# First tile of attention and FFN: rows two to four normalised on GpSimd, row four's attention products earlier, ScalarE's splits ahead of a test

## The chip, the core and the metric

The kernel runs on one core of one Trainium2 chip. The metric is the device time of one execution in microseconds (us), median over runs. The core has TensorE (matrix products), VectorE, ScalarE and GpSimd (elementwise work) and SyncE, which here only issues DMAs. The engines run their own instruction lists in order and wait for one another on semaphores.

## The reference

One block over x of 8 x 256 tokens x 256 features, float32:

```
q = layernorm(x)                                   # no learned scale
scores = q @ ctx.T / 16, causal, padded keys masked with -inf
x = x + softmax(scores) @ ctx
n = layernorm(x)
h = silu(n @ w1.T * s1) * (n @ w2.T * s2)          # 256 -> 1024, weights -1, 0, 1
h = gelu(h @ h1.T * sh1);  h = gelu(h @ h2.T * sh2)  # 1024 -> 1024, twice
out = x + h @ w3.T * s3                            # 1024 -> 256
```

## The kernel before, in words

The 2048 tokens are four tiles of 512, each of two sequences of 256. A tile has four "rows" of 128 tokens (r = 0 to 3 in the code; "row one" to "row four" in words); rows 0 and 1 are the first sequence. All 22 weight pieces (128 x 1024 each) stay in SBUF. The FFN's activations are split into a high and a low part, and each weight multiplies both in two matmuls, so the hidden layers take most of TensorE.

The four tiles run one after another on TensorE. In tiles 2 to 4 the attention of the next tile is slipped between hidden chunks. The first tile has nothing to be slipped into, so it has a path written out by hand: the functions whose names begin with `first_`, and the order of their calls on each engine. That order is what the change edits.

For one row of the first tile: statistics of x (`first_stats_of`, `first_moments_of`), deviation, transpose, scores, exponentials, transposed probabilities, the product with the context (`first_attend`, TensorE, line 1180), division by the row sum and addition of x (`first_attention`, VectorE, line 779), statistics and moments again (lines 727, 732), the reciprocal root of the variance on GpSimd (`first_attention_rstd`, lines 402 and 403), normalisation (`first_normalise`, VectorE, line 791), transpose (`first_turn_xn`, TensorE, line 1188), the high part on ScalarE and the low part on VectorE (both `first_split`, lines 510 and 798). Then gate and up products start (`gate_and_up`, line 997). In the first tile the first chunks are done for the first sequence alone (batch 0, 256 columns), then for the second (batch 1). The PSUM banks form a ring of six: chunk 3 needs the banks of chunk 0 and so waits until VectorE has multiplied gate and up of chunk 0 (line 819), which waits for ScalarE's silu (line 549).

Beside that, ScalarE tests every weight piece for bits that a shorter format would lose (`test_piece`, line 466). TensorE sums the test results (`sum_flag`, line 1063), VectorE reduces them to a flag (`take_flag`, line 804), and TensorE's queue loads the flag and branches (`segment`) before the products of the segment: GATE_UP_A ahead of the first product, then GATE_UP_B, HID1A, HID1B, HID1C and LAST. The first six pieces arrive in buffers that are free at first (gate, residual, ctx_cols, work, turned, ctx_rows) and GpSimd copies them into the weights' place (`first_weights`, line 436). SyncE issues raw pieces 4 and 5 when row four's attention product is done (`first_attended[3]`), the next tile's queries when VectorE has added the fourth row (`x_attn_done`), and then the stream of the other pieces, each staged in DRAM and then loaded.

`stay_busy(n)` issues n matmuls on zeros into a bank that nobody reads. Between them stand waits.

Of the kernel before, what the change touches and what calls it, by code (L numbers as in the profile page):

```python
# [20 lines left out]
ALU = mybir.AluOpType  # L21
# [7 lines left out]
PAIR = 2  # L29
# [21 lines left out]
GATE_UP_A, GATE_UP_B, HID1A, HID1B, HID1C, LAST = range(6)  # L51
# [7 lines left out]
def xattn_ffn(nc, x, x_cols_d, ctx_rows_d, ctx_cols_d, mask_d, weights_d, scales_d, down_scale_d, out):  # L59
# [7 lines left out]
    with stack:  # L67
# [13 lines left out]
        x_attn = sb("x_attn", [P, ROWS, EMB])  # L81
# [18 lines left out]
        mean_var = sb("mean_var", [P, ROWS, 2])  # L100
# [266 lines left out]
        def _(pool):  # L367
# [53 lines left out]
            def first_attention_rstd(r):  # L421

                pool.wait_ge(first_moments, ROWS + r + 1)
                rstd_of(slice(r, r + 1)).then_inc(first_rstd, 1)

            def first_mask_of(b):

                if b == 0:
                    pool.wait_ge(mask_loaded, 16)
                nc.gpsimd.tensor_scalar(first_mask[:, b], mask[0:1, b, 0:SEQ].bitcast(I32), 0.0, MASKED,  # L430
                                        ALU.is_equal, ALU.mult).then_inc(first_masked, 1)
# [10 lines left out]
            first_weights(0)  # L442
            first_attention_rstd(0)
            first_attention_rstd(1)
            pool.wait_ge(first_xn[1], 1)
            first_weights(1)
            first_attention_rstd(2)
            first_attention_rstd(3)
            pool.wait_ge(first_xn[3], 1)
            for n in range(2, RAW):  # L450
                first_weights(n)
            for t in range(1, TILES):
# [6 lines left out]
        def _(act):  # L459
            def test_piece(n):  # L460

                act.wait_ge(raw_in[n] if n < RAW else loaded[n], 16)
                if n:
                    act.wait_ge(low_summed, n)
                low = (raw_pieces[n] if n < RAW else weights[:, n]).bitcast(U16)[:, 0:2 * PIECE:2]
                nc.scalar.activation(test_out, low, ACT.Copy, accum_out=low_sums[:, n:n + 1]  # L466
                                     ).then_inc(low_summed, 1)
# [39 lines left out]
            def first_split(r):  # L507

                act.wait_ge(first_xn_turned[r], 1)
                nc.scalar.activation(xn_hi[:, :, r * P:(r + 1) * P],  # L510
                                     first_bank[r][:, 0:EMB].rearrange("p (c t) -> p c t", c=EC), ACT.Copy
                                     ).then_inc(first_xn_hi[r], 1)
# [77 lines left out]
            def load_table(n, function):  # L590
                nc.scalar.activation(table_out[:, n:n + 1], zero_col[:], function)
# [19 lines left out]
            first_split(0)  # L611
            first_split(1)
            test_piece(2)
            test_piece(3)
            first_split(2)
            first_split(3)
            load_table(1, ACT.Silu)
            act.wait_ge(scales_in, 16)

# [12 lines left out]
        def _(dve):  # L632
# [292 lines left out]
            first_inverse(1)  # L925
            first_normalise(0)
            first_attention(2)
            first_normalise(1)
            first_attention_stats(2)
            take_flag(GATE_UP_A)  # L930
            first_moments_of(2, 1)
            first_split(0)
            first_split(1)
            first_attention(3)
            first_attention_stats(3)
            first_moments_of(3, 1)
            first_normalise(2)
            first_normalise(3)
            first_split(2)
            first_split(3)  # L940
            dve.wait_ge(scales_in, 16)
# [7 lines left out]
        def _(pe):  # L949
# [116 lines left out]
            def first_tile():  # L1066
                def batches(dt):

                    pe.wait_ge(first_copied, 1)
                    gate_and_up(0, (0, 1), dt, 0)  # L1070
                    first_turn_xn(2)
                    stay_busy(2)
                    first_turn_xn(3)
                    pe.wait_ge(first_copied, 2)
                    gate_and_up(0, (2,), dt, 0)
                    gate_and_up(0, (0,), dt, 1)
                    sum_flag(GATE_UP_B)
                    gate_and_up(0, (1, 2), dt, 1)
                    gate_and_up(0, (3,), dt)

                def remaining(dt):

                    pe.wait_ge(first_copied, GU_P)
                    gate_and_up(0, (4, 5, 6), dt)
                    sum_flag(HID1A)
                    gate_and_up(0, (7,), dt)

                def hid1(flag, *chunks, inner=None):

                    if flag == HID1A:  # L1090
                        pe.wait_ge(first_copied, RAW)
                    segment(flag, lambda dt: hidden(0, 0, chunks, dt, inner))

                segment(GATE_UP_A, batches)
                segment(GATE_UP_B, remaining)
                hid1(HID1A, 0)
                hid1(HID1A, 1, inner=HID1B)
                hid1(HID1B, 2, 3, 4)
                hid1(HID1B, 5, inner=HID1C)
                hid1(HID1C, 6, 7)  # L1100
                scores(1)
                segment(HID1C, lambda dt: hidden(0, 1, range(0, 3), dt))
                segment(HID1C, lambda dt: hidden(0, 1, (3,), dt, LAST))
                segment(LAST, all_tested)
# [106 lines left out]
            first_attend(1)  # L1211
            first_attend(2)
            first_turn_probs(3)
            stay_busy(9)
            first_turn_xn(0)
            stay_busy(2)
            pe.wait_ge(ones_made, 1)
            sum_flag(GATE_UP_A)
            stay_busy(1)
            first_turn_xn(1)  # L1220
            first_attend(3)
            first_tile()


# [35 lines left out]
```

## Time and profile before

| | us |
|---|---|
| median of 3 runs | 363.0 |
| lowest, highest | 362.63, 363.38 |
| profiled execution, time | 363.59 |
| profiled execution, span | 361.8 |
| TensorE busy | 356.6 (99%) |
| VectorE busy | 181.8 (50%) |
| ScalarE busy | 147.6 (41%) |
| GpSimd busy | 35.8 (10%) |

The span runs from the first instruction of the kernel to the last. The granted TensorE clock was 1.0 throughout. Shares of busy time are averages over the whole span: VectorE is busy half of it, but in the first 25 us nearly all of the time.

### The profile page before, as it was taken

To read this page: it belongs to the slowest core of one execution; us is meant where nothing else is said; L and a number is where in the kernel's file an instruction comes from. 1 tells how busy PE (TensorE), PEld (TensorE's weight loads), DVE (VectorE), ACT (ScalarE), POOL (GpSimd) and SP (SyncE) were. 2 spreads that over 40 slices of the span, in tenths; PEclk is the share of its full clock that TensorE was granted. 3 is DMA by queue.
4 is the path that set the end of the run, shared out by engine and by line. 5 is a ranking of instruction groups with operands and counts; after the bars stand their busy time and mean duration, and the time that the engine had idled before them with its cause. 6 is when DMAs were issued, how large, how long until landed. Compare 5 with 4: busy or idle time off the path is not lost.

```text
span 361.8 us, 4628 instructions
## 1 busy us (share of the span) xinstructions
PE 356.6 (99%) x1746; PEld 300.9 (83%) x1746; DVE 181.8 (50%) x402; ACT 147.6 (41%) x247; POOL 35.8 (10%) x59
## 2 busy tenths in 40 slices
PE   8999999999999999999999999999999999999996
PEld 7888787888898888888898888888889888888886
DVE  3859326435648764338345845335626662323233
ACT  4789953761136622521143641621123652212120
POOL 7450103100100220001000050001000000000000
PEclk9999999999999999999999999999999999999999
DMA  7799989969269000210833010030411000000001
GB/s 253 276 380 416 408 316 377 432 153 356 59 136 350 12 29 0 67 22 11 206 108 112 3 29 0 21 68 0 94 23 47 14 1 0 2 0 0 2 0 62
DMA packets 39569, 43.82 MB, mean 121 GB/s; under 512 B 23746, under 2 KB 32068, under 8 KB 39364
## 3 DMA queue, kind: packets, MB, share of 16 engines
q1 hardware_dynamic: 38672, 42.62, 35.2%
q10 hardware_dynamic: 868, 0.80, 0.8%
q8 instruction: 20, 0.33, 0.4%
q14 instruction: 9, 0.07, 0.1%
HBM read 38.55 MB, written 16.39 MB: 152 GB/s over the span
## 4 chain that ended last, share of the span: by engine, by line
PE 98%; DVE 0%; ACT 0%; issue 0%
PE ring L1025 65%; PE ring L997 16%; PE ring L1044 8%; PE att L957 2%; PE att L969 2%; PE ring L1134 2%; PE ring L1180 0%; PE ring L1143 0%; PE att L1161 0%; PE ring L1161 0%; ACT act L569 0%; PE ring L1188 0%; PE att L1188 0%; PE att L1063 0%; PE ring L1151 0%
## 5 line engine op out<-in xcount | busy, mean ns | idle before, releaser
L1025 PE MATMUL ring<-h_hi,weights 128*128 128x512 f32 x512 | 201.2, 393 | 0.8 <-ACT act L569 0.8
L1025 PE MATMUL ring<-h_lo,weights 128*128 128x512 f32 x512 | 199.6, 390 | 0.0
L1025 PEld LDWEIGHTS ring<-h_hi,weights 128*128 128x128 f32 x512 | 96.1, 188 | 22.0 <-ACT act L569 1.2
L1025 PEld LDWEIGHTS ring<-h_lo,weights 128*128 128x128 f32 x512 | 96.2, 188 | 19.7
L569 ACT ACTIVATE act<-ring,scales 128x512 f32<-128x512 f32 x64 | 44.1, 688 | 155.7 <-PE ring L1025 155.5
L838 DVE CAST h_hi<-act 128x512 fp32r<-128x512 f32 x64 | 27.5, 429 | 123.1 <-ACT act L569 123.0
L722 DVE TENSOR_TENSOR h_lo<-act,h_hi 128x512 fp32r<-128x512 f32 x96 | 66.5, 693 | 2.3
L997 PE MATMUL ring<-xn_hi,weights 128*128 128x512 f32 (+1 forms) x140 | 51.6, 375 | 0.2 <-DVE xn_lo L798 0.2
L997 PE MATMUL ring<-xn_lo,weights 128*128 128x512 f32 (+1 forms) x140 | 51.2, 372 | 0.0
L549 ACT ACTIVATE gate<-ring,scales 128x512 f32<-128x512 f32 x32 | 22.0, 688 | 26.3 <-PE ring L997 26.3
L1044 PE MATMUL ring<-weights,h_lo 128*128 128x256 f32 x128 | 30.9, 283 | 0.0
L1044 PE MATMUL ring<-weights,h_hi 128*128 128x256 f32 x128 | 30.9, 283 | 0.0
L997 PEld LDWEIGHTS ring<-xn_hi,weights 128*128 128x128 f32 x140 | 26.3, 188 | 5.3 <-POOL weights L436 0.5
L997 PEld LDWEIGHTS ring<-xn_lo,weights 128*128 128x128 f32 x140 | 26.4, 189 | 4.4
L819 DVE SCALAR_TENSOR_TENSOR act<-ring,scales,gate 128x512 f32<-128x512 f32 x32 | 24.0, 749 | 12.0 <-PE ring L997 9.9
L1044 PEld LDWEIGHTS ring<-weights,h_lo 128*128 128x128 f32 x128 | 24.6, 192 | 0.2
L1044 PEld LDWEIGHTS ring<-weights,h_hi 128*128 128x128 f32 x128 | 24.5, 192 | 0.2
L539 ACT ACTIVATE h_hi<-act 128x512 fp32r<-128x512 f32 x32 | 20.0, 626 | 2.0 <-DVE act L819 2.0
L466 ACT ACTIVATE scaled<-weights 128x1024 bf16<-128x1024 uint16 x16 | 16.8, 1053 | 3.6 <-DMA weights<-weights_staged 2.9
L402 POOL TENSOR_SCALAR var_eps<-mean_var 128x4 f32<-128x4 f32 (+2 forms) x12 | 2.4, 199 | 104.4 <-DVE mean_var L647 101.6
L851 DVE TENSOR_TENSOR scaled<-ring,down_scale 128x256 f32<-128x256 f32 x16 | 6.8, 422 | 7.3 <-PE ring L1044 7.3
L569 ACT ACT_TABLE_LOAD x7 | 9.0, 1283 | 2.7 <-POOL mean_scaled L409 2.6
(125 smaller groups left out, 215.2 us busy)
## 6 DMA issues: line engine op xcount, KB each, us to landing
weights<-weights_staged SPq DMA_DIRECT2D x11, 1024.0 KB, 8.8
x_in<-in_x SPq DMA_DIRECT2D x8, 256.0 KB, 4.6
ctx_cols<-in_ctx_cols SPq DMA_DIRECT2D x8, 256.0 KB, 5.4
ctx_rows<-in_ctx_rows SPq DMA_DIRECT2D x4, 512.0 KB, 6.9
out_dram<-residual SPq DMA_DIRECT2D x16, 128.0 KB, 2.0
turned<-in_x_cols SPq DMA_DIRECT2D x3, 512.0 KB, 8.4
xn_blocks<-work SPq DMA_DIRECT2D x3, 512.0 KB, 3.2
turned<-xn_blocks SPq DMA_DIRECT2D x12, 128.0 KB, 2.8
```

The source lines that it names most:

```text
L466: nc.scalar.activation(test_out, low, ACT.Copy, accum_out=low_sums[:, n:n + 1]).then_inc(low_summed, 1)
L539: nc.scalar.activation(h_hi[0][:, c], act32[:, c % 3], ACT.Copy).then_inc(hi_done, 1)
L549: nc.scalar.activation(gate[:, c % 2], ring[2 * c % RING][:], ACT.Silu, scale=gate_scale[:, c:c + 1]).then_inc(gate_done, 1)
L569: nc.scalar.activation(act32[:, n % 3], ring[(2 * HC + HC * layer + c) % RING][:], ACT.Gelu, scale=scale[:, c:c + 1]).then_inc(gelu_done, 1)
L722: nc.vector.tensor_tensor(h_lo[buf][:, c], act32[:, n % 3], h_hi[buf][:, c].bitcast(F32), op=ALU.subtract).then_inc(split, 1)
L819: nc.vector.scalar_tensor_tensor(out=act32[:, c % 3], in0=ring[(2 * c + 1) % RING][:], scalar=up_scale[:, c:c + 1], in1=gate[:, c % 2], op ...
L838: nc.vector.tensor_copy(h_hi[buf][:, c], act32[:, n % 3]).then_inc(hi_made, 1)
L957: ins = nc.tensor.matmul(att[b][:, cols], q_cols[:, b, c, q * P:(q + 1) * P], ctx_cols[:, b, c, 0:(q + 1) * P], start=(c == 0), stop=(c == ...
L969: ins = nc.tensor.matmul(att[b][:, q * EMB:(q + 1) * EMB], later_probs_t[:, b, n * P:(n + 1) * P], ctx_rows[:, 2 * b + k], start=(k == 0), ...
L997: ins = nc.tensor.matmul(bank[:, toks], w, part[:, k, toks].bitcast(dt), start=(k == 0 and part is xn_hi), stop=(k == EC - 1 and part is x ...
L1025: ins = nc.tensor.matmul(bank[:], w, part[:, k].bitcast(dt), start=(k == 0 and part is h_hi[src]), stop=(k == HC - 1 and part is h_lo[src]))
L1044: ins = nc.tensor.matmul(bank[:, 0:EMB], part[:, k, r * P:(r + 1) * P].bitcast(dt), w, start=(k == 0 and part is h_hi[0]), stop=(k == last ...
```

## The change

On GpSimd a new function `first_normalise(r)` does with `tensor_scalar` what VectorE's function of that name does. GpSimd runs it for rows 1, 2 and 3, each behind that row's reciprocal root; two waits of GpSimd on VectorE's normalisation go. VectorE keeps row 0 only, and its `take_flag(GATE_UP_A)` moves behind the first split. ScalarE does the splits of rows 2 and 3 ahead of the test of piece 3. TensorE does row 3's attention product ahead of row 0's transpose, with other counts of `stay_busy`, and row 2's transpose between the first two chunks.

```diff
@@ gpsimd @@
+            def first_normalise(r):
+
+                pool.wait_ge(first_rstd, PAIR + r + 1)
+                nc.gpsimd.tensor_scalar(xn_first[:, r], x_attn[:, r], mean_var[:, r, 0:1], rstd[:, r:r + 1],
+                                        ALU.subtract, ALU.mult).then_inc(first_xn[r], 1)
...
             first_attention_rstd(1)
-            pool.wait_ge(first_xn[1], 1)
+            first_normalise(1)
+            first_attention_rstd(2)
+            first_normalise(2)
             first_weights(1)
-            first_attention_rstd(2)
             first_attention_rstd(3)
-            pool.wait_ge(first_xn[3], 1)
+            first_normalise(3)
@@ scalar @@
             test_piece(2)
-            test_piece(3)
             first_split(2)
             first_split(3)
+            test_piece(3)
@@ vector @@
             first_attention(2)
-            first_normalise(1)
             first_attention_stats(2)
-            take_flag(GATE_UP_A)
             first_moments_of(2, 1)
             first_split(0)
+            take_flag(GATE_UP_A)
             first_split(1)
             first_attention(3)
             first_attention_stats(3)
             first_moments_of(3, 1)
-            first_normalise(2)
-            first_normalise(3)
@@ tensor, first gate/up batches @@
-                    gate_and_up(0, (0, 1), dt, 0)
+                    gate_and_up(0, (0,), dt, 0)
                     first_turn_xn(2)
-                    stay_busy(2)
+                    gate_and_up(0, (1,), dt, 0)
+                    stay_busy(1)
                     first_turn_xn(3)
@@ tensor, ahead of them @@
             first_turn_probs(3)
-            stay_busy(9)
+            stay_busy(6)
+            first_attend(3)
             first_turn_xn(0)
             stay_busy(2)
...
             first_turn_xn(1)
-            first_attend(3)
+            stay_busy(4)
             first_tile()
```

## Rows read from the trace of the kernel before

**Rows 1.** Chain of waits in order of time: start us, us, what.

```profile
17.14 2.15 PE ring L997 x16
...
55.70 1.04 PE ring L1025 x4
...
56.76 0.70 ACT act L569
...
57.48 7.54 PE ring L1025 x32
```

**Rows 2.** Timeline, 52 to 57 us: start, us, engine, line, what, [idle before <-releaser].

```profile
52.45 1.06 ACT L466 ACTIVATE scaled<-weights 128x1024 bf16<-128x1024 uint16 x1 [2.50 <-DMA weights<-weights_staged]
...
56.53 0.14 DVE L804 TENSOR_REDUCE seg_flags<-att 1x1 f32<-1x6 f32 x1
```

**Rows 3.** Timeline of VectorE, 15 to 20 us.

```profile
15.85 0.13 DVE L804 TENSOR_REDUCE seg_flags<-ring 1x1 f32<-1x2 f32 x1
...
16.07 0.90 DVE L798 TENSOR_TENSOR xn_lo<-ring,xn_hi 128x256 fp32r<-128x256 f32 x2
17.00 0.48 DVE L779 SCALAR_TENSOR_TENSOR x_attn<-att,inv_sum,x_in 128x256 f32<-128x256 f32 x1
...
17.98 0.18 DVE L732 BATCH_NORM_AGGREGATE mean_var<-stats 128x2 f32<-128x6 f32 x1
...
19.26 0.41 DVE L791 TENSOR_SCALAR act<-x_attn,mean_var,rstd 128x256 f32<-128x256 f32 x1 [0.78 <-POOL rstd L403]
```

**Rows 4.** Timeline of TensorE and its weight loads, 13 to 25 us.

```profile
13.37 1.31 PE L1134 MATMUL ring<-h_lo 128*128 128x256 f32 x9
14.64 0.44 PE L1188 MATMUL ring<-ident,act 128*128 128x128 f32 x2
...
15.67 0.43 PE L1188 MATMUL ring<-ident,act 128*128 128x128 f32 x2
15.93 1.03 PE L1180 MATMUL att<-ctx_rows,turned 128*128 128x256 f32 x4
...
19.73 0.44 PE L1188 MATMUL att<-ident,act 128*128 128x128 f32 x2
...
21.10 0.39 PE L997 MATMUL ring<-xn_hi,weights 128*128 128x256 f32 x1
...
24.45 0.19 PEld L997 LDWEIGHTS ring<-xn_hi,weights 128*128 128x128 f32 x1 [0.21 <-DVE act L819]
```

**Rows 5.** Timeline of ScalarE and VectorE, 20 to 25 us.

```profile
20.20 0.38 ACT L510 ACTIVATE xn_hi<-att 128x256 fp32r<-128x256 f32 x1 [0.27 <-PE att L1188]
20.61 1.28 ACT L591 ACT_TABLE_LOAD   x1
...
22.44 0.69 ACT L549 ACTIVATE gate<-ring,scales 128x512 f32<-128x512 f32 x1 [0.34 <-PE ring L997]
...
23.65 0.75 DVE L819 SCALAR_TENSOR_TENSOR act<-ring,scales,gate 128x512 f32<-128x512 f32 x1 [0.95 <-PE ring L997]
24.84 0.75 DVE L819 SCALAR_TENSOR_TENSOR act<-ring,scales,gate 128x512 f32<-128x512 f32 x1 [0.45 <-ACT gate L549]
```

**Rows 6.** Timeline of GpSimd, 14 to 19 us.

```profile
14.53 0.55 POOL L403 TENSOR_TENSOR rstd<-var_eps,minus_half 128x1 f32<-128x1 f32 x1
...
18.25 0.27 POOL L402 TENSOR_SCALAR var_eps<-mean_var 128x1 f32<-128x1 f32 x1 [0.65 <-DVE mean_var L732]
18.61 0.54 POOL L403 TENSOR_TENSOR rstd<-var_eps,minus_half 128x1 f32<-128x1 f32 x1
```

**Rows 7.** Groups of GpSimd by line and shape, whole span: busy us, mean ns | idle.

```profile
L393 POOL TENSOR_SCALAR mask<-mask 128x512 f32<-128x512 int32 x3 | 6.5, 2152 | 21.8 <-DMA mask<-in_mask 21.8
...
L436 POOL CAST weights<-residual 128x1024 fp32r<-128x1024 f32 x1 | 1.0, 1036 | 0.6 <-DVE act L791 0.6
...
L383 POOL TENSOR_SCALAR_AFFINE_SELECT tri<-tri 128x256 f32<-128x256 f32 x1 | 0.4, 411 | 0.1
```

**Rows 8.** Timeline of SyncE, 16 to 18 us: issues of DMAs.

```profile
16.99 0.33 SPq L311 DMA_DIRECT2D turned<-in_weights  x1
```

## The prediction

> **What bounds the kernel now.** I read the chain of waits first. From the first gate/up product at 17.14 us to the end TensorE is practically never idle, so a microsecond is won or lost only by moving that first product, or by a gap among the products behind it. The chain shows one such gap of any size: it leaves TensorE for ScalarE at 56.76 and comes back at 57.48 [rows 1]. The four products before it end at 55.70 + 1.04 = 56.74, so it is 0.74 us. The name there is misleading: chunk 6 of the first hidden layer needs gelu 1, long done. What it needs is the flag that VectorE takes at 56.53 to 56.67 [rows 2], and between a flag and the first product behind it lie 0.81 us here and 1.16 us at the first segment (flag done 15.98, product 17.14) [rows 1, 3]: load, test, branch. The flag is late because VectorE takes it behind the split of a gelu, which on ScalarE stands behind two weight tests that waited 2.50 us for a DMA [rows 2].
>
> Then the timeline up to 25 us, one engine at a time. Two more places are tight: row four's transpose, which started at 19.73 just after its normalisation ended (19.26 + 0.41) [rows 3, 4], with batch 1 following at 21.10; and chunk 3, whose weight load at 24.45 waited 0.21 us for the gated chunk 0 of VectorE (23.65 + 0.75) [rows 4, 5]. I number the rows of the tile one to four as the change does.
>
> **The change, part by part.**
>
> *Fourth row's attention moved up.* Before row one's transpose there now stand six fillers instead of nine and four attention matmuls. A filler costs 0.12 us (nine span 1.31 with a tail of about 0.2 [rows 4]); the four take 0.85 (1.03 less the tail [rows 4]). The fillers end at 14.1, the attention at about 14.95, and row one's transpose starts at 15.0 instead of 14.64: 0.37 later. Its other side, the 0.85 taken from behind row two's transpose, bought nothing before: the product then waited for row two's split anyway [rows 3]. From row one's to row two's transpose is 1.03 us, from there to the product 1.47 [rows 1, 4], both unchanged in work: 17.5. The flag now stands behind row one's split on VectorE: 15.0, 0.46 to ScalarE's part, 0.42 to VectorE's, 0.43 for it and 0.15 for the flag make 16.46, and with the 1.16 from flag to product 17.6. The first product starts at about **17.6, 0.45 later**.
>
> *Row two normalised on GpSimd.* It can begin behind the reciprocal root, at 14.53 + 0.55 + 0.08 = 15.16 [rows 6], and is wanted at 16.03. Anything under 0.85 us is hidden by the later transpose.
>
> *What the GpSimd operation costs.* The trace of before has no float tensor-by-two-scalars of this size there; VectorE takes 0.41 [rows 3]. From below: a one-input select of 128x256 floats took 0.41, and a cast of 1024 columns 1.04, that is about 0.8 ns a column. From above: the same opcode on 512 int32 columns took 2.15, 4.2 ns a column, so 1.07 for 256 [rows 7]. A float input is nearer to the first two rows, and there is one more arithmetic step; I take **0.50**, an estimate. GPSIMD Engine Reference of the Trainium skill, section "Performance versus the Vector engine", puts a body of at most two steps at 1.03 cycles per element and gives about 1.8 as the best case of a tight unrolled loop; with its 1.2 GHz and 0.2 us of start (this trace's smallest operations) that is an estimate of 0.42 to 0.58, by which the sum would move by 0.08 either way, while the same page's rule to leave elementwise work to VectorE stands against the change. No row here decides between them.
>
> *Row four's normalisation.* VectorE's order is now split one, flag, split two, attention four. Before, attention four started at 17.00 right behind the two splits [rows 3]; split two now ends 0.37 later (transpose 16.03), so attention four, its statistics and moments all shift by 0.37, the moments to 18.35 to 18.53. GpSimd has by then done norm two (15.66), root three and norm three (17.15) and copied piece 1 (18.2), so it is free. From the end of the moments to row four's transpose was 1.57 us (18.16 to 19.73) [rows 3, 4], of which VectorE's 0.41 becomes 0.50 with one hand-over less. I keep 1.60: transpose four at **20.12, 0.39 later**. TensorE gets there by 19.9 (17.6, chunk 0 at 0.99, transpose three, chunk 1 at 0.99, one filler), so the normalisation sets it. Behind GpSimd's new waits are queued the copies of pieces 2 to 5, four of 1.04: the last ends near 24.3 as before, and its product comes at 34. Batch 1 is 1.37 behind it [rows 4]: 21.49.
>
> *Splits ahead of a test.* The old test 3 waited for its piece and ended before row three's split was wanted. Now test 3 (1.05, as in [rows 2]) stands between the last split and the table load (1.28), then the small activation, then the first silu. Before, split 20.20, table 20.61, activation 21.90 to 22.10, and silu at 22.44 had waited 0.34 for TensorE [rows 5]. Now split four starts at 20.12 + 0.47 = 20.59, test 21.00, table 22.05, silu possible at 23.57 (table end 23.33, 0.2 and a hand-over): 1.13 later, where TensorE would be only 0.39 later. ScalarE becomes what is late. Silu 0.70, VectorE's product 0.76 and two hand-overs of 0.1 make the gated chunk ready at 25.15, and chunk 3 starts at **25.2, 0.75 later** (24.45 before). I assume that the 0.5 us which VectorE let pass before its 23.65 start (silu done 23.13 [rows 5]) doesn't come back; if it does, 0.42 is added. The silus behind it run 1.1 us late. Chunk 4, due 1.83 us behind chunk 3, had its bank free at 24.84 + 0.75 = 25.6 [rows 5] and began at 26.3: 0.7 to spare, of which 1.1 - 0.75 is used up, so no second stall.
>
> *Earlier loads.* SyncE waited for attention four before raw pieces 4 and 5, at 16.99 [rows 8]; it will issue them near 15.2. The queries of the next tile wait for VectorE's addition, 0.37 later. The DMA stream of the weights so starts its backlog over a microsecond earlier, and the pieces tested at 52.45 land earlier.
>
> *The sum.* 0.75 us late into the hidden layer. At 56.7 the old gap of 0.74 takes it up: if the flag comes no earlier than before, TensorE arrives at 57.49 where it once waited until 57.48. Net 0.75 - 0.74 = **0.0 us**. The profiled execution has a span of 361.8 and 363.59 in all, 0.6 above the median 363.0 of the runs; the difference is applied to the median: **363.0**.
>
> **Rivals.**
>
> *A: GpSimd is slow on this operation (it ends slower).* At 1.07 us row two is ready at 16.3, 0.2 late, norm three ends at 18.3, the copy of piece 1 at 19.35, and only then come root four (0.9) and norm four: 21.45, transpose four at 21.5 instead of 19.73. Up to 0.7 us a tenth of duration costs a tenth; from there it costs three, since three normalisations stand in one queue. Transpose four 1.75 late, chunk 3 0.36 more: 2.1; less 0.74 is +1.4: 364.4. For it the int32 row, against it the select and the cast. At 0.8 it is +0.5.
>
> *B: the gap at 56.7 doesn't take the delay up.* VectorE's flag is itself moved by 0.75, because gelu and splits are late with TensorE and ScalarE, or the weight DMA behind the later addition: +0.74, 363.7. Against it: the tests there waited for a DMA, not for TensorE. The 0.42 of the gated chunk gives 363.4 in the same way.
>
> *C: the DMA stream wins.* The pieces for the tests at 52.45 land over a microsecond earlier, the flag no longer lags, the gap goes whole, and ScalarE's lateness at the first silu is less than I add up (0.35 in place of 0.75): -0.4, 362.6; with the small waits at 21.10 and 24.45 gone too and normalisation at 0.41, -0.8: 362.2.
>
> *D: it does nothing at all*, because first product and chunk 3 keep their times: 0.74 of gap may still go or stay; it lies within the forecast's own bounds.
>
> **How the numbers follow.** A measurement of this kernel can tell about 0.2% from no change, 0.73 us: 362.3 to 363.7. Forecast 0.50 (nearly all "same"); A 0.22 (nearly all slower); B 0.14 (half slower); C and D 0.14, of which 0.09 is beyond the bound. With the forecast's tails: faster 0.12, same 0.58, slower 0.30. Range 362.3 to 364.4, from the middle of C to A.
>
> **What would show it.** GpSimd's tensor-scalar at 0.5 us (above 0.7: A); first product at 17.6; transpose four near 20.1; silu at 23.6, chunk 3 near 25.2; the gap at 57 gone and the products behind it at 57.5. If chunk 3 stands by 24.8, ScalarE's queue was mis-sized; if the gap is still 0.7, B.

## The result and the profile after

| | before | changed |
|---|---|---|
| median, us | 363.38 (13 runs) | 365.62 (13 runs) |
| lowest, highest | 362.28, 365.09 | 364.83, 368.15 |
| ratio | | 1.0072 [1.0052, 1.0092] |
| profiled execution: time, span | 363.59, 361.8 | 365.52, 363.6 |

The change makes the kernel slower by 0.7%, about 2.2 us. The forecast was no change, and 365.62 lies above its range. What happened is its rival A, and more of it than the 364.4 that the rival was given.

GpSimd's new operation, by its own line (duration in ns, minimum, median, maximum):

```profile
L429 POOL TENSOR_SCALAR act<-x_attn,mean_var,rstd x3: 1223/1228/1231, 14.9 to 20.4; 128x256 f32<-128x256 f32 x3
```

It takes 1.23 us, where VectorE's took 0.41 [rows 3] and the forecast said 0.50. The timeline of GpSimd after (start, us, what), which answers to [rows 6]:

```profile
14.20 0.55 POOL L403 TENSOR_TENSOR rstd<-var_eps,minus_half 128x1 f32<-128x1 f32 x1
14.86 1.23 POOL L429 TENSOR_SCALAR act<-x_attn,mean_var,rstd 128x256 f32<-128x256 f32 x1
...
17.11 1.23 POOL L429 TENSOR_SCALAR act<-x_attn,mean_var,rstd 128x256 f32<-128x256 f32 x1
18.29 1.04 POOL L442 CAST weights<-residual 128x1024 fp32r<-128x1024 f32 x1
19.41 0.19 POOL L402 TENSOR_SCALAR var_eps<-mean_var 128x1 f32<-128x1 f32 x1
19.68 0.56 POOL L403 TENSOR_TENSOR rstd<-var_eps,minus_half 128x1 f32<-128x1 f32 x1
20.36 1.22 POOL L429 TENSOR_SCALAR act<-x_attn,mean_var,rstd 128x256 f32<-128x256 f32 x1
```

From 14.86 to row four's normalisation GpSimd is idle only for hand-overs of about 0.1 us. VectorE had row four's moments at 18.54 (below), but its root began at 19.41, when the queue was free. VectorE after, answering to [rows 3]:

```profile
17.38 0.47 DVE L786 SCALAR_TENSOR_TENSOR x_attn<-att,inv_sum,x_in 128x256 f32<-128x256 f32 x1
...
18.36 0.18 DVE L739 BATCH_NORM_AGGREGATE mean_var<-stats 128x2 f32<-128x6 f32 x1
```

TensorE after, answering to [rows 4]: row one's and row two's transpose, the first product, row three's transpose, and row four's, which waited 1.54 us for GpSimd.

```profile
14.75 0.38 PE L1193 MATMUL ring<-ident,act 128*128 128x128 f32 x2
...
16.15 0.44 PE L1193 MATMUL ring<-ident,act 128*128 128x128 f32 x2 [0.44 <-POOL act L429]
...
17.61 0.36 PE L1001 MATMUL ring<-xn_hi,weights 128*128 128x256 f32 x1 [0.55 <-DVE xn_lo L805]
...
18.64 0.38 PE L1193 MATMUL att<-ident,act 128*128 128x128 f32 x2
...
21.63 0.44 PE L1193 MATMUL att<-ident,act 128*128 128x128 f32 x2 [1.54 <-POOL act L429]
```

The chain of waits after, answering to [rows 1] (start, us, what). It no longer stays on TensorE: it runs through GpSimd to row four's transpose, then through ScalarE's test (new at this place) and table load ahead of the first silu (line 556), and VectorE, to chunk 3 at 26.53, against 24.45 before.

```profile
20.36 1.23 POOL act L429
21.59 0.04 issue
21.63 0.45 PE att L1193 x2
...
22.39 1.14 ACT scaled L473 x2
23.55 0.75 ACT L598
...
25.04 0.59 ACT gate L556
25.72 0.76 DVE act L826
26.48 0.04 issue
26.53 7.56 PE ring L1001 x32
...
58.33 8.54 PE ring L1029 x36
...
66.87 2.62 PE att L961 x16
```

The last rows show the gap near 57 us gone: 36 products stand in one piece. VectorE has taken the flag as soon as TensorE had summed it, where in [rows 2] it was late:

```profile
58.37 0.15 DVE L811 TENSOR_REDUCE seg_flags<-att 1x1 f32<-1x6 f32 x1 [0.97 <-PE att L1067]
```

So chunk 3 is 2.08 us late on the profile's own clock. 0.5 more comes at the start of the first hidden layer: the product behind the flag sum at 58.33 is 2.63 later than the 55.70 of before. 0.78 comes back at the gap: the next stage starts at 66.87, 1.85 behind 65.02, and VectorE's last operation is 1.85 late too. In this profile the first tile began 0.33 us earlier than in the one of before (row two's root at 14.20 against 14.53), so the delay from there on is 1.85 + 0.33 = 2.18 us, which is what the timed runs show (2.2).

SyncE issued raw piece 4 at 14.95, 2.0 us earlier than in [rows 8]:

```profile
14.95 0.33 SPq L311 DMA_DIRECT2D turned<-in_weights  x1
...
17.88 0.81 SPq L246 DMA_DIRECT2D x_in<-in_x  x2
```

### The profile page after: what moved, and what is told of

Its sections match the earlier page's. It is cut to its first block, busy times and chain, and to the rows that moved or that the text cites. A ratio compares the mean times of both kernels' runs of the same rounds, so it can differ in the third digit from the quotient of the medians.

```text
span 363.6 us, 4623 instructions
## 1 busy us (share of the span) xinstructions
PE 356.3 (98%) x1746; PEld 300.3 (83%) x1746; DVE 181.7 (50%) x399; ACT 147.0 (40%) x247; POOL 39.1 (11%) x62
## 4 chain that ended last, share of the span: by engine, by line
PE 95%; POOL 2%; DVE 1%; ACT 1%; issue 1%; DVEq 0%; ACTq 0%
PE ring L1029 64%; PE ring L1001 15%; PE ring L1048 8%; PE att L961 2%; PE att L973 2%; PE ring L1139 1%; POOL act L429 1%; POOL rstd L403 0%; PE ring L1166 0%; ACT scaled L473 0%; PE ring L1185 0%; POOL weights L442 0%; PE ring L1148 0%; DVE neg_max L765 0%; DVE act L826 0%
## 5 line engine op out<-in xcount | busy, mean ns | idle before, releaser
L409 POOL TENSOR_SCALAR mean_scaled<-mean_var 128x4 f32<-128x4 f32 x3 | 1.3, 423 | 86.0 <-DVE mean_var L654 86.0
```

## The experiments

The profiled executions begin their first tile at different times: row two's root (line 403, 128x1, its second row) starts between 13.47 and 15.00 us, whatever was edited. So besides the timed ratio I use a measure from each profile: the time from that start to the start of the last VectorE operation, less that of before (359.25 - 14.53 = 344.72). I call it the stretch. For the changed kernel it is 361.10 - 14.20, +2.18 us. (In e13 and e14 the start is taken 0.27 earlier, since a small operation of 0.27 with its hand-over stands ahead of the root there.)

The stretch has a weakness, the gap near 57 us. e10_price and e12_price_forms are the kernel before with operations added at the end of GpSimd's list alone, so up to there they are the same kernel. The gap was 0.74 us in the profile of before, 0.70 in e10_price and 0.07 in e12_price_forms. It hangs on how long the first of two weight tests waited for its DMA: 2.50, 2.45 and 1.33 us. In e12_price_forms:

```profile
51.08 1.06 ACT L479 ACTIVATE scaled<-weights 128x1024 bf16<-128x1024 uint16 x1 [1.33 <-DMA weights<-weights_staged]
...
55.54 0.15 DVE L817 TENSOR_REDUCE seg_flags<-att 1x1 f32<-1x6 f32 x1 [0.30 <-PE att L1076]
```

```profile
55.50 1.02 PE ring L1038 x4
...
56.59 7.54 PE ring L1038 x32
```

So a stretch 0.7 below before is what the unchanged kernel gives too, in an execution without the gap, and one profile can't show that an edit closed it. The last column of the table leaves the gap out: the stretch less that kernel's gap, less the same of before (344.72 - 0.74 = 343.98). There e10_price and e12_price_forms stand within 0.03 us of before.

| kernel | ratio to before, 95% | median, us | stretch, us | gap, us | stretch without the gap, us |
|---|---|---|---|---|---|
| changed | 1.0072 [1.0052, 1.0092] | 365.62 | +2.18 | 0 | +2.92 |
| after_again | 1.0049 [1.0026, 1.0072] | 365.76 | +2.27 | 0.07 | +2.94 |
| e1_vector_norm | 1.0009 [0.9986, 1.0031] | 363.77 | +0.31 | 0 | +1.05 |
| e2_only_gpsimd | 1.0039 [1.0015, 1.0064] | 365.32 | +1.69 | 0.08 | +2.35 |
| e3_only_splits | 1.0009 [0.9983, 1.0035] | 364.08 | -0.02 | 0.13 | +0.59 |
| e4_only_attention | 0.9978 [0.9958, 0.9998] | 363.15 | -0.65 | 0 | +0.09 |
| e5_row4_vector | 1.0065 [1.0040, 1.0090] | 365.63 | +1.57 | 0.08 | +2.23 |
| e6_test_back | 1.0045 [1.0017, 1.0072] | 365.14 | +1.48 | 0 | +2.22 |
| e7_flag_earlier | 0.9984 [0.9968, 1.0000] | 362.72 | -0.65 | 0 | +0.09 |
| e9_attention_between | 0.9988 [0.9970, 1.0006] | 362.67 | -0.77 | 0.07 | -0.10 |
| e10_price (one run) | | 364.99 | -0.05 | 0.70 | -0.01 |
| e11_both | 0.9983 [0.9957, 1.0008] | 362.80 | -0.90 | 0 | -0.16 |
| e12_price_forms (one run) | | 362.69 | -0.70 | 0.07 | -0.03 |
| e13_quick_form | 1.0029 [1.0006, 1.0052] | 364.60 | +0.63 | 0 | +1.37 |
| e14_quick_test_back | 1.0003 [0.9978, 1.0028] | 363.72 | +0.09 | 0.07 | +0.76 |

The kernel before had medians of 363.54 (e1 to e4), 363.01 (e5 to e10), 363.53 (e6, again, e11, e12) and 363.15 (e13, e14) beside them.

**The whole change but GpSimd.** Against the changed kernel:

```diff
@@ gpsimd @@
-            first_normalise(1)
+            pool.wait_ge(first_xn[1], 1)
+            first_weights(1)
             first_attention_rstd(2)
-            first_normalise(2)
-            first_weights(1)
             first_attention_rstd(3)
-            first_normalise(3)
+            pool.wait_ge(first_xn[3], 1)
@@ vector @@
             first_attention(2)
+            first_normalise(1)
             first_attention_stats(2)
...
             first_moments_of(3, 1)
+            first_normalise(2)
+            first_normalise(3)
```

> The changed kernel with rows two to four normalised on VectorE again, at their old places; the earlier attention product, the splits ahead of the test and the flag behind the first split stay. Theory Q (GpSimd's queue is the cause: three operations of 1.23 us in place of 0.42, with the copy of piece 1 between the second and the third): row four's transpose comes back from 21.6 to about 20.1 us, chunk 3 from 26.5 to about 25.2, the gap near 57 us stays gone, and the time is that of before, ratio 0.999 to 1.002. Rival S (ScalarE's order or the earlier attention product is the cause): it stays at 1.005 or above.

Measured: no difference from before that can be told. In its profile row four's transpose starts at 19.74 and chunk 3 at 25.00, where it waited 0.60 us for VectorE, whose operation waited for ScalarE's silu:

```profile
19.74 0.38 PE L1195 MATMUL att<-ident,act 128*128 128x128 f32 x2
...
25.00 0.50 PE L1003 MATMUL ring<-xn_hi,weights 128*128 128x512 f32 x1 [0.60 <-DVE act L825]
```

Theory Q holds: without GpSimd's three operations the loss is gone. This kernel also shows the rest of the forecast at work: without the gap it is 0.87 us late up to 65 us, where the forecast had 0.75, and 0.74 of that comes back since it has no gap. (0.18 more lies behind 65 us, in tiles that no edit touched.)

**GpSimd alone.** The kernel before with GpSimd's new list, as in the change, and without the three operations on VectorE.

```diff
@@ vector @@
             first_attention(2)
-            first_normalise(1)
             first_attention_stats(2)
...
             first_moments_of(3, 1)
-            first_normalise(2)
-            first_normalise(3)
```

> The kernel before with only the normalisation of rows two to four moved to GpSimd, in the changed kernel's GpSimd order. Theory Q: row two is ready at about 16.4 us, row four's transpose at about 21.9 (19.73 before), batch 1 at 23.2, chunk 3 near 26.6, of which the gap near 57 us gives 0.74 back: +1.4 us, ratio 1.004 (1.003 to 1.007). Rival S: within 0.2% of before.

Measured 1.0039, inside the expected bounds. GpSimd's part alone is most of the loss: +2.35 of +2.92 us without the gap. Counted from row two's root, row four's transpose came 7.43 us behind it (20.97 - 13.54), as in the changed kernel (21.63 - 14.20), against 5.20 before.

**ScalarE's order alone.**

```diff
             test_piece(2)
-            test_piece(3)
             first_split(2)
             first_split(3)
+            test_piece(3)
```

> The kernel before with only ScalarE's order changed (splits of rows three and four ahead of the test of piece 3). Theory Q: the splits stay at 19.55 and 20.20 us, the test stands between them and the table load, silu 0 at about 23.2 (22.44 before), chunk 3 at about 24.8 to 24.9 (+0.4); the gap near 57 us, set by VectorE's flag behind a DMA, takes it up: ratio 1.000 (0.999 to 1.001). Rival S: 1.003 or more, since ScalarE runs late through the whole first layer.

Its chain (before: chunk 3 at 24.45, behind the gap at 57.48):

```profile
25.07 7.58 PE ring L997 x32
...
57.50 7.53 PE ring L1025 x32
```

Chunk 3 came 0.62 late, 0.2 more than expected, and behind the gap the difference was 0.02. VectorE took the flag at the same time as before (56.54), so the gap took the delay up, as the forecast said. It could, because this execution had the late flag: the test there had waited 1.87 us for its DMA. The timed ratio can't tell 0.6 us of delay from none.

**TensorE's order alone.**

```diff
-                    gate_and_up(0, (0, 1), dt, 0)
+                    gate_and_up(0, (0,), dt, 0)
                     first_turn_xn(2)
-                    stay_busy(2)
+                    gate_and_up(0, (1,), dt, 0)
+                    stay_busy(1)
                     first_turn_xn(3)
...
-            stay_busy(9)
+            stay_busy(6)
+            first_attend(3)
             first_turn_xn(0)
...
             first_turn_xn(1)
-            first_attend(3)
+            stay_busy(4)
             first_tile()
```

> The kernel before with only TensorE's order changed (row four's attention product ahead of row one's transpose, six and four fillers, row three's transpose between the first chunks). Theory Q: first product at about 17.5 us (17.14 before), row four's transpose at about 20.0, batch 1 at 21.4, chunk 3 at about 24.7; raw pieces 4 and 5 issued near 15.2; the gap near 57 us shrinks or goes: ratio 0.998 to 1.001. Rival S: 1.002 or more.

Measured 0.9978, with an interval that ends just short of 1.0: this part alone is no loss and may be a gain of 0.2%. Counted from row two's root (14.85, 0.32 later than before in this execution) the first product is 0.15 late and chunk 3 0.15 late, and the gap is gone:

```profile
17.61 0.35 PE L997 MATMUL ring<-xn_hi,weights 128*128 128x256 f32 x1 [0.53 <-DVE xn_lo L798]
...
24.92 0.50 PE L997 MATMUL ring<-xn_hi,weights 128*128 128x512 f32 x1
```

```profile
56.18 8.52 PE ring L1025 x36
```

SyncE issued raw piece 4 at 15.60, 1.7 us earlier by the same count, and the two tests had no wait for a DMA. That agrees with the forecast's earlier loads as what closes the gap. But e12_price_forms had no gap either, without any edit, so one profile doesn't show it. Without the gap TensorE's order costs 0.09 us.

**Row four back on VectorE, rows two and three on GpSimd.**

```diff
@@ gpsimd @@
             first_attention_rstd(3)
-            first_normalise(3)
+            pool.wait_ge(first_xn[3], 1)
@@ vector @@
             first_moments_of(3, 1)
+            first_normalise(3)
```

> The changed kernel with row four alone normalised on VectorE again; rows two and three stay on GpSimd. Theory Q (a queue of three operations and a copy on GpSimd): row four's root still ends at 20.2 us behind norm three and the copy of piece 1, VectorE's operation takes 0.42 in place of 1.23, transpose four at 20.8 (21.63 in the changed kernel), chunk 3 near 25.7; span about 362.8, ratio to the kernel before 1.003 (1.001 to 1.005). Rival (only the last operation counts): ratio 1.000 to 1.001.

In the profile the transpose came at 20.72 and chunk 3 at 25.62, as expected, and the stretch is 0.61 shorter than in the changed kernel. So it isn't the last operation alone: with that one back on VectorE, most of the loss stays. The time didn't follow. The ratio, 1.0065, lies above the expected bounds; it rests on six executions, from 364.59 to 366.81. In the profiled one 4.0 us pass between the end of VectorE's last operation (360.80) and the end of the span (364.8), against 2.1 to 2.2 in every other profile here but e10_price. That tail is no part of what was edited, and the stretch leaves it out.

**The flag a step earlier, in the kernel before.**

```diff
-   ((HID1B, (0, 0)), (HID1C, (0, 5)), (LAST, (1, 3)))
+   ((HID1B, (0, 0)), (HID1C, (0, 4)), (LAST, (1, 3)))
```

> The kernel before with one edit behind the first layer: VectorE takes the flag of segment HID1C ahead of the split of gelu 4 instead of behind it. Theory F (the gap of 0.74 us near 57 us is the flag's, standing behind a split that stands behind tests waiting for a DMA): the flag is done near 55.9, the gap goes, ratio 0.998 (0.997 to 0.999). Rival (the gap is ScalarE's gelu, as the chain of waits names it): no change, 1.000.

Chain and VectorE's row:

```profile
55.65 8.53 PE ring L1025 x36
```

```profile
55.69 0.15 DVE L804 TENSOR_REDUCE seg_flags<-att 1x1 f32<-1x6 f32 x1 [4.60 <-PE att L1063]
```

The gap is absent in this profile, and the median is 0.3 us lower, with an interval that ends at 1.0. The profile doesn't show that the edit did it: the test waited 0.70 us for its DMA here, where in e12_price_forms 1.33 was short enough to have no gap without the edit. Without the gap the stretch differs from before by +0.09, all of it behind 65 us.

That the gap is the flag's and not ScalarE's, as the chain of waits named it, is shown by other rows. Where VectorE took the flag late, the next product started 0.80 to 0.82 us behind the flag's end: 57.48 before, 57.06 in e10_price (flag done 56.26), 57.50 in e3_only_splits (flag done 56.68). And in e12_price_forms the product started at 56.59, while the gelu that the chain names ran until 57.25; it can't have waited for it.

**Row four's addition between the first two splits**, on top of e4_only_attention.

```diff
             first_split(0)
+            first_attention(3)
             first_split(1)
-            first_attention(3)
             first_attention_stats(3)
```

> The kernel before with TensorE's order of the change (as in e4_only_attention) and, on VectorE, row four's attention addition between the first two splits. Theory Q: VectorE idles there for the second split, so the addition costs 0.1 to 0.2 us at the first product and brings row four's moments about 0.5 us earlier; row four's transpose no longer waits, SyncE's loads for the next tile start earlier; ratio 0.997 to 0.999. Rival (first product alone counts): 1.000.

Chunk 3 came 9.79 us behind row two's root (23.36 - 13.57), against 10.07 in e4_only_attention and 9.92 before. In the times it can't be told from e4_only_attention or from before.

**Both edits together.** e9_attention_between with e7_flag_earlier's line.

> The two edits that helped, together: TensorE's order of the change with row four's addition between the first two splits (as e9_attention_between), and the flag of HID1C ahead of the split of gelu 4 (as e7_flag_earlier). In the profiles of both the gap near 57 us was already gone, so they share it and don't add up. Theory: 0.9975 to 0.9985 of before, no more than either alone by 0.1%. Rival (they are worth 0.4% together): 0.996.

The gap was already gone in the profile of each, and together they bring no more: 0.9983, an interval that takes in 1.0. The ratios of e4, e7, e9 and e11 are 0.9978 to 0.9988, a gain of 0.1% to 0.2% at the edge of what this measurement tells.

**Only ScalarE's order undone, and the change again.** The edit is that of e3_only_splits reversed, in the changed kernel.

> The changed kernel with only ScalarE's order undone (test of piece 3 ahead of the splits of rows three and four). With transpose four at 21.6 us the test has ended by 19.5, so the table load follows the last split at 22.5, silu 0 can start at 24.3 (24.95 in the changed kernel) and chunk 3 at 26.0 to 26.2 (26.53), TensorE itself being ready near 26.0. Theory P (ScalarE's order adds to GpSimd's cost once the gap near 57 us no longer hides it): 0.4 to 0.9 us less than the changed kernel, its ratio to before 1.003 to 1.005. Rival (it is hidden behind row four's wait for GpSimd): the same as the changed kernel within 0.2 us.

> The changed kernel once more, on the chip of this set: 1.005 to 1.009 of the kernel before, with GpSimd's normalisation at 1.23 us three times and transpose four about 6.8 us behind the start of norm two.

Chunk 3 stood 11.98 us behind row two's root (26.05 - 14.07) against 12.33 in the changed kernel (26.53 - 14.20); the stretch is 0.70 shorter. The medians, 365.14 and 365.76, differ the same way, but their intervals overlap. The rival is not excluded by the times, only by the profiles. The change again came out at 1.0049, just under what was expected, with three operations of 1.22 to 1.23 us.

**What the operation costs, by itself.** Sixteen GpSimd operations at the end of its list (eight forms, two rounds), each waited for before the next and by no other engine. The first of the eight, with its loop:

```diff
+            for _ in range(2):
+                chain(nc.gpsimd.tensor_scalar(priced[:], source, mean_var[:, 0, 0:1], rstd[:, 0:1], *two))
```

> The kernel before with sixteen extra operations at the end of GpSimd's list, each waited for, on a tile nobody reads, so that the price of one is seen by itself: the normalisation's form on 256 and on 128 columns, the same two steps with immediates, multiply and add with immediates, one multiply with a per-partition scalar, one with an immediate, the int32 form, a copy. Theory Q: the normalisation's form takes 1.23 us on 256 columns and about 0.7 on 128, so about 4 ns a column, as the int32 rows of before had it, whatever the input type; a copy takes 0.4. Rival: the price comes from the per-partition scalars, and the forms with immediates take about 0.5.

Second round of its timeline: the normalisation's form, 128 columns of it, subtract-multiply and multiply-add with immediates, and the int32 form:

```profile
261.07 1.54 POOL L461 TENSOR_SCALAR priced<-tri,mean_var,rstd 128x256 f32<-128x256 f32 x1
262.72 0.79 POOL L462 TENSOR_SCALAR priced<-tri,mean_var,rstd 128x128 f32<-128x128 f32 x1
263.60 1.07 POOL L463 TENSOR_SCALAR priced<-tri 128x256 f32<-128x256 f32 x1
264.75 0.59 POOL L464 TENSOR_SCALAR priced<-tri 128x256 f32<-128x256 f32 x1
...
267.38 1.08 POOL L467 TENSOR_SCALAR priced<-tri 128x256 f32<-128x256 int32 x1
```

The normalisation's form took 1.39 and 1.54 us here (first and second round), more than its 1.23 in the first tile, and 0.79 on 128 columns, so 256 columns cost nearly twice as much. The rival is wrong: without per-partition scalars the form still takes 1.07. Floats with a subtraction at 1.07 and int32 with a comparison at 1.08: a float input, by which the forecast chose, doesn't make the form quick. Whether int32 with a quick pair would be quick wasn't run. And multiply-add took 0.59, which neither theory had; by the starts of the operations it is 0.69 against 1.15. So other pairs were run:

> The kernel before with sixteen extra GpSimd operations on a tile nobody reads, other forms of tensor-by-two-scalars on 256 float columns: multiply-add and multiply-subtract with per-partition scalars, add-multiply, multiply-multiply and multiply-subtract with immediates, and 128 columns of two forms. Theory G (multiply then add alone is quick, by the 0.58 us it took with immediates against 1.07 for subtract then multiply): multiply-add with per-partition scalars near 0.75 us, all other pairs 1.0 to 1.5. Rival (a leading multiply is what is quick): multiply-multiply and multiply-subtract also near 0.6.

Second round: multiply-add and multiply-subtract with per-partition scalars; add-multiply, multiply-multiply and multiply-subtract with immediates.

```profile
258.98 0.56 POOL L461 TENSOR_SCALAR priced<-tri,rstd,mean_var 128x256 f32<-128x256 f32 x1
259.64 1.23 POOL L462 TENSOR_SCALAR priced<-tri,rstd,mean_var 128x256 f32<-128x256 f32 x1
260.96 0.50 POOL L463 TENSOR_SCALAR priced<-tri 128x256 f32<-128x256 f32 x1
261.55 0.41 POOL L464 TENSOR_SCALAR priced<-tri 128x256 f32<-128x256 f32 x1
262.04 1.07 POOL L465 TENSOR_SCALAR priced<-tri 128x256 f32<-128x256 f32 x1
```

Theory G is wrong, since add-multiply and multiply-multiply are quick too, and so is its rival, since multiply-subtract is slow. What the slow float pairs have in common is a subtraction, in either place. Pairs of multiply and add take 0.41 to 0.68, those with a subtraction 1.07 to 1.54.

**The change with the quick form.** The same normalisation without a subtraction.

```diff
+                if r:
+                    nc.gpsimd.tensor_scalar(neg_mean[:, r:r + 1], mean_var[:, r, 0:1], -1.0, 0.0, ALU.mult, ALU.add
+                                            ).then_inc(pool_step, 1)
+                    steps[0] += 1
                 rstd_of(slice(r, r + 1)).then_inc(first_rstd, 1)
...
-                nc.gpsimd.tensor_scalar(xn_first[:, r], x_attn[:, r], mean_var[:, r, 0:1], rstd[:, r:r + 1],
-                                        ALU.subtract, ALU.mult)
+                nc.gpsimd.tensor_scalar(xn_first[:, r], x_attn[:, r], neg_mean[:, r:r + 1], rstd[:, r:r + 1],
+                                        ALU.add, ALU.mult)
```

> The changed kernel with GpSimd's normalisation of rows two to four written as (x + (-mean)) * rstd in place of (x - mean) * rstd, and a small operation of about 0.2 us that makes -mean ahead of each root. Theory V (the price of subtract-multiply carries most of the loss): one normalisation takes 0.6 to 0.7 us in place of 1.23, transpose four comes 1.0 to 1.2 us earlier than in the changed kernel (6.3 us behind the root of row two in place of 7.4), and the time falls by about 1.1 us, to 1.001 to 1.003 of before. Rival (the hand-over to GpSimd costs it, not the operation; or per-partition scalars make add-multiply slow too): 1.005 or more.

```profile
20.09 0.56 POOL L434 TENSOR_SCALAR act<-x_attn,neg_mean,rstd 128x256 f32<-128x256 f32 x1
```

The operation takes 0.56, a little under what was expected, on the kernel's own data and in its own place. The stretch falls by 1.55 to +0.63, the time to 1.0029 from 1.0072 and 1.0049. The pair of arithmetic steps in this one form carries 1.5 of the 2.2 us, although each row pays 0.27 for the negated mean.

**And ScalarE's order of before with it.**

> e13_quick_form with ScalarE's order of before (test of piece 3 ahead of the splits of rows three and four). Theory V with the second term (ScalarE's order costs 0.5 to 0.9 us once nothing behind hides it): 0.4 to 0.9 us below e13_quick_form, 0.999 to 1.001 of before. Rival (ScalarE's order is free): equal to e13_quick_form within 0.2 us.

Measured 1.0003, and +0.09 in the stretch; the second term is 0.54 there and 0.88 us in the medians, whose intervals overlap. With both, the kernel is as fast as before. But this undoes ScalarE's order, which the forecast had in its sum, so it is not the change as forecast.

## Why the prediction was wrong, point by point

- **The price of GpSimd's operation (the step that failed).** The text put 0.50 between 0.41 and 1.07 because "a float input is nearer" to the select and the cast [rows 7]. It measured 1.23, above even the upper bound. The row of the same opcode was the nearer one in size. It was so partly by luck: its first operation is a comparison and the normalisation's a subtraction, and the same opcode took 0.41 to 0.59 with other pairs. A subtraction on floats costs 1.07 with immediates (e10_price), and per-partition scalars add 0.15 to 0.47. The forecast took a price from rows of another opcode, and gave the row of the same opcode a chance of 0.22.
- **Its leverage.** Rival A had it right: beyond 0.7 us a tenth costs three tenths, since norm two, norm three, the copy and norm four share one queue. It was worked out for 1.07 and gave transpose four at 21.5 and chunk 3 at +2.1, and the profile has 21.63 and +2.08. That these agree is luck, since the price was 1.23 and the tile began 0.33 early. With 0.16 more at three to one, rival A has transpose four 7.4 us behind row two's root (7.43 measured), chunk 3 at +2.6 (12.33 less 9.92 is +2.41) and a sum of +1.9, where the stretch has +2.18; the rest is the hidden layer's 0.5, below.
- **Everything else of the sum** can be read in e1_vector_norm, counted from row two's root. Transpose four: 5.59 forecast, 5.46 measured. Silu 0: 9.04 against 8.72. Chunk 3: 10.67 against 10.72. The last is two misses that cancel: the silu was possible 0.3 earlier than forecast, but the 0.5 us that VectorE lets pass behind it, which the forecast assumed would not come back, came back (silu done 23.67, VectorE's start 24.19). It came back in e3_only_splits too and not in the changed kernel (0.10); why isn't shown. Net: 0.0 forecast, +0.31 in the stretch and 1.0009 in time.
- **First product**: forecast 17.6, measured 17.61, again by luck. Row two's transpose waited 0.44 us for GpSimd and the tile began 0.33 early; from the root it is 3.41 us where the forecast had 3.07. In e1_vector_norm it is 3.14, and there the product did wait for the flag, as the forecast said it would (flag done 16.28, product 17.42, split two done 16.90).
- **VectorE's load**: the text on the profile before has VectorE busy "nearly all of the time" in the first 25 us. It was busy for 14.06 of them (56%), TensorE for 23.65, and ahead of row four's normalisation it sat idle for 0.78 us [rows 3]. So taking three operations from it relieved no full engine.
- **The gap near 57 us**: that it is the flag's, and that it takes up a delay, is shown (0.80 to 0.82 us from flag to product in three profiles; 0.62 taken up in e3_only_splits). What the forecast missed is that the kernel before has it in some executions and not in others: 0.74, 0.70 and 0.07 us in three profiles of the same code. So the 0.74 in its sum was the figure of one execution. That the earlier loads close it, as rival C had it, fits the profiles and isn't shown.
- **ScalarE's order**: the forecast had it as 0.36 us at chunk 3 (0.75 against TensorE's 0.39) and called the silus behind it harmless. It costs 0.5 to 0.7 us where the gap doesn't hide it: e13 to e14 0.54, changed to e6 0.70 in the stretch. From row two's root to the first hidden product the two pairs differ by 0.53 and 0.49, so most of it is there by then. e4_only_attention to e1_vector_norm is +0.96, but that pair also moves the flag behind the first split (first product 0.38 later, transpose four 0.05) and has the 0.18 behind 65 us in it.
- **Not in the forecast**: 0.5 us at the start of the first hidden layer. From the last gate/up product to the second weight load below 3.91 us passed before (37.58 - 33.67) and 4.43 after (40.18 - 35.75). Before, then after:

```profile
37.58 0.19 PEld L1025 LDWEIGHTS ring<-h_hi,weights 128*128 128x128 f32 x1 [0.31 <-issue]
```

```profile
35.01 0.13 DVE L811 TENSOR_REDUCE seg_flags<-att 1x1 f32<-1x2 f32 x1
```

```profile
36.15 0.19 PEld L1029 LDWEIGHTS ring<-h_hi,weights 128*128 128x128 f32 x1 [0.43 <-DVE act L826]
...
40.18 0.19 PEld L1029 LDWEIGHTS ring<-h_hi,weights 128*128 128x128 f32 x1 [0.52 <-issue]
```

  0.2 of it is the first load, which had no wait before. It is named after VectorE's gated chunk (line 826), but that was done at 35.80, 0.35 ahead. What ended 1.01 us ahead of the load is the flag of this segment (35.01 + 0.13), and in all seven profiles in which this load waited it came 1.00 to 1.02 us behind that flag's end. TensorE had summed the flag from 33.92 on; VectorE, late with the gated chunks because the silus are late, took it at 35.01. So the lateness that the forecast called harmless comes out here, by the same way as at the gap near 57 us. Another 0.2 is the second load, behind the next load of a flag and its branch, and 0.1 lies in the products between. My reading of the second is that TensorE's queue, late itself at 36.15, has no lead left there to hide the branch; this was not tested by itself and stays open.

By the stretch without the gap, each part alone costs: TensorE's order 0.09, ScalarE's order 0.59, GpSimd 2.35. The sum is 3.03, and the whole change has 2.92; the gap gives 0.74 of it back, +2.18.

## What to carry to other kernels

Where one operation moves to another engine, and a range of two to one hangs on its price, measure that very form first, at the end of the engine's list where nobody waits for it, as e10_price does. The estimate from other opcodes was off by a factor of 2.5 here, and the row of the same opcode, near by luck, would have been as far off for a pair of multiply and add. Then count how often the price stands in one queue: here a miss of 0.7 us in one operation cost 1.9 us. In this kernel, writing a subtraction in a GpSimd tensor-by-two-scalars as an addition of the negated scalar took the operation from 1.23 to 0.56 us, for a small operation of 0.27 ahead of it. A wait that the chain names after one engine may be another's, and a gap that hangs on a DMA may be there in one execution and gone in the next: read it in more than one profile of the unchanged kernel before a sum rests on it or an edit is said to close it.

## What the runs showed of the hardware

- GpSimd's tensor-by-two-scalars on 128 x 256 floats: 0.41 to 0.59 us for pairs of multiply and add with immediates (0.56 to 0.68 with per-partition scalars), 1.07 to 1.12 with a subtraction and immediates, 1.23 to 1.54 with a subtraction and per-partition scalars (e10_price, e12_price_forms, e13_quick_form). int32 with a comparison: 1.08 to 1.09. One multiply alone took 0.85 to 0.97, more than the quick pairs. On 128 columns subtract-multiply took 0.79 to 1.00, so the price isn't in proportion to the columns for every form. The cycles per element in GPSIMD Engine Reference of the Trainium skill, section "Performance versus the Vector engine", from which the prediction worked out its estimate of 0.42 to 0.58 for this size, agree with the quick pairs and are off by more than two for those with a subtraction, on which the measurements decide.
- Price and place: 1.23 in the first tile three times within 8 ns, 1.39 to 1.54 at the end of the list for the same form. The source tile and what the other engines did beside it differ as well; why wasn't looked into.
- Between the end of a flag's reduction and the first product behind its branch lie 0.80 to 0.82 us where the product waited for the flag near 57 us (before, e3_only_splits, e10_price), and 1.14 at the first segment of e1_vector_norm (16.28 to 17.42), and 1.00 to 1.02 to the first weight load of the hidden layer in the seven profiles in which it waited. A flag taken just in time is taken late. The 1.16 that the prediction read at the first segment of before is no such case: split two ended at 16.97, 0.17 ahead of that product.
- The same code waited 2.50, 2.45 and 1.33 us for one weight DMA in three profiles (before, e10_price, e12_price_forms), which opened a gap of 0.74, 0.70 and 0.07 us in TensorE's products.
